# A graph network on one core: SyncE also fetches one tile in 48 of the pair pass, by one-row transfers into four slots of their own

## The reference

```python
h = jnp.maximum(_layernorm(x, axis=-1), 0.0)
hihj = jnp.concatenate([x[src], x[dst]], axis=-1)                       # x is h in here
exp_e = jnp.exp(_silu(_bn(hihj @ Wf + bf, f_gamma, f_beta)))
we = weight[src] * exp_e
a = we / segment_sum(we, dst, num_segments=N)[dst]
z = jnp.einsum('ed,hdk->ehk', hihj, Wg) + bg
z = _silu(_bn(z, g_gamma, g_beta))
h = segment_sum((a[:, :, None] * z).reshape(E, -1), dst, num_segments=N)
out = _bn(h, n_gamma, n_beta) + x
```

## Time and profile before

| | |
|---|---|
| median of 3 runs | 11156.53 us (11154.51 to 11157.13) |
| the profiled execution | 11159.11 us |
| its span, first to last instruction | 11157.3 us |
| GpSimd busy over the span | 8098.3 us, 73% |
| PE, PEld, VectorE, ScalarE busy | 4270.1, 2948.2, 3430.3, 3212.6 us |
| mean granted TensorE clock | 0.596 |
| the gathers of the three passes in parts | 4596, busy 4348.0 us |
| of the pass with weights | 1532, busy 1454.6 us |
| of the pair pass | 1563, busy 1496.6 us |

### The profile page before, as it was taken

One profiled execution on the slowest core, in us unless ns is written; L12 is line 12 of the kernel. 1 busy time (PEld: TensorE's weight loads), 2 busy tenths in 40 slices (PEclk: granted clock), 3 DMA queues, 4 the chain that ended last, 5 costly groups with the idle time before them and its releaser, 6 DMA issues. The chain is left out here.

```text
span 11157.3 us, 112702 instructions
## 1 busy us (share of the span) xinstructions
PE 4270.1 (38%) x19462; PEld 2948.2 (26%) x19462; DVE 3430.3 (31%) x7386; ACT 3212.6 (29%) x7261; POOL 8098.3 (73%) x8241
## 2 busy tenths in 40 slices
PE   1222222342222233333333433343464333443687
PEld 0111111121111112111111333333353333333576
DVE  4000001110001112000001422222245677777898
ACT  3333333343333334333333300000031111111465
POOL 4777777657777775777777677777766777777676
PEclk5555555665555555555555555556675555555899
DMA  4333333233333333333333222222214555555444
GB/s 105 81 81 81 81 81 81 76 88 81 81 81 81 81 81 102 81 81 81 81 81 81 59 54 54 54 54 54 54 48 148 159 162 163 166 166 170 149 167 134
DMA packets 702798, 1071.72 MB, mean 96 GB/s; under 512 B 164740, under 2 KB 547065, under 8 KB 675209
## 3 DMA queue, kind: packets, MB, share of 16 engines
q0 software_dynamic: 323616, 664.87, 23.0%
q10 hardware_dynamic: 247712, 225.10, 6.1%
q1 hardware_dynamic: 130793, 174.77, 4.9%
HBM read 904.67 MB, written 161.05 MB: 96 GB/s over the span
## 5 line engine op out<-in xcount | busy, mean ns | idle before, releaser
L460 POOL DMA_INDIRECT big<-table_parts,tile_cols x4596 | 4348.0, 946 | 1563.2 <-issue 1400.2
L641 PE MATMUL psum<-big 128*128 x4992 | 1722.0, 505 | 3998.4 <-SPq L472 3044.2
L641 PEld LDWEIGHTS psum<-big 128*128 128x128 bf16 x4992 | 670.0, 141 | 4980.6 <-issue 2814.6
L460 POOL DMA_INDIRECT big<-ptable,tile_cols x1563 | 1496.6, 957 | 498.4 <-issue 476.0
L460 POOL DMA_INDIRECT big<-table,tile_cols x1532 | 1454.6, 949 | 469.5 <-issue 467.0
L596 ACT ACTIVATE big<-big,ones 128x2048 bf16<-128x2048 bf16 x312 | 624.4, 2001 | 3573.5 <-PE psum L641 2381.1
L589 ACT ACTIVATE big<-iota_col,dl_tab 128x128 bf16<-128x128 f32 x4992 | 1490.7, 387 | 32.9 <-PEq L765 12.5
L1656 PE MATMUL psum<-acc,big 128*128 x3328 | 785.0, 419 | 1205.5 <-DVE big L1632 1193.4
L618 DVE TENSOR_REDUCE acc<-psum 128x128 f32<-128x384 f32 (+1 forms) x196 | 109.7, 560 | 3558.1 <-PE psum L644 1783.4
L713 PE MATMUL psum<-big 128*128 x3328 | 754.6, 419 | 1158.3 <-SPq L472 619.7
L1656 PEld LDWEIGHTS psum<-acc,big 128*128 128x128 f32 x3328 | 701.8, 315 | 1288.5 <-issue 1288.2
(11 more groups left out here) (301 smaller groups left out, 4278.8 us busy)
## 6 DMA issues: line engine op xcount, KB each, us to landing
big<-table_parts SPq DMA_DIRECT2D x11904, 0.8 KB
big<-dl_rows ACTq DMA_DIRECT2D x104, 1024.0 KB
zrows<-big ACTq DMA_DIRECT2D x104, 1024.0 KB, 5.5
big<-zrows SPq DMA_DIRECT2D x104, 1024.0 KB, 4.9
big<-table_parts,tile_cols POOLq DMA_INDIRECT x4596
big<-table SPq DMA_DIRECT2D x3968, 0.5 KB
table_parts<-big SPq DMA_DIRECT2D x42, 672.0 KB, 3.5
big<-ptable,tile_cols POOLq DMA_INDIRECT x1563
```

The lines of the kernel that those rows point to most:

```text
L460: pool.indirect_dma_start(out=slots[:, t % (groups * GT), 0:width], out_offset=None, in_=tab, in_offset=bass.IndirectOffsetOnAxis(ap=idx_t ...
L641: last = nc.tensor.matmul(held, m, rows_t, start=False, stop=False, skip_group_check=True)
```

## The change

The pair pass, too, gives the last tile of every sixth group to SyncE. Its list, `Z_SIDE`, has 32 groups (8 to 194), one more than `SIDE`, since the ring is shorter. The row numbers are copied a third time into `side_tab` and multiplied by 520, the bytes of a row of `ptable`. A fetched tile does not go into the ring but into one of four slots of its own, `z_side`, which lie behind the work buffer in `big`, at `Z_SIDE_AT`. So the table of slots needs other entries for the items of these tiles: nine further small operations of VectorE in setup find whether a tile is a fetched one (a division by 48 by a multiplication and a shift), which of the four slots it has, and add the difference to `slot_at`. VectorE then addresses all of `big` with the table. The relaying, the ring and the passes 0 to 3 stay.

```diff
+    Z_SIDE = list(range(SIDE_FIRST, TGROUPS - Z_RGROUPS + Z_LEAD + 1, SIDE_EVERY))
+    Z_SIDE_SLOTS, SIDE_TILES = 4, SIDE_EVERY * GT
+    SIDE_SHIFT, SIDE_FACTOR, SIDE_FROM = 16, -(-(1 << 16) // SIDE_TILES), 2
+    SIDE_OFFSET = SIDE_FROM * SIDE_TILES - SIDE_FIRST * GT - GT + 1
...
+        Z_SIDE_AT = RB + OB + WB
+        z_side = big[:, Z_SIDE_AT:Z_SIDE_AT + Z_SIDE_SLOTS * ACW].rearrange("p (u f) -> p u f", f=ACW)
...
-        side_tab = sb("side_numbers", [64 + len(SIDE), P], i32)
-        side_of = [side_tab[64 * k:64 * k + len(SIDE), :] for k in range(2)]
+        side_tab = sb("side_numbers", [64 + len(Z_SIDE), P], i32)
+        side_of = [side_tab[32 * k:32 * k + len(Z_SIDE), :] for k in range(3)]
...
-            return no < PASSES - 1 and g in SIDE
+            return g in (SIDE if no < PASSES - 1 else Z_SIDE)
...
-                if k >= len(SIDE):
+                if k >= len(SIDE if no < PASSES - 1 else Z_SIDE):
                     return
-                t = SIDE[k] * GT + GT - 1
+                t = Z_SIDE[k] * GT + GT - 1
+                slot = t % RSLOTS if no < PASSES - 1 else (k + SIDE_FROM) % Z_SIDE_SLOTS
...
-                    sp.dma_start(slots[e:e + 1, t % RSLOTS, 0:width], flat[:, bass.ds(at, width)]).then_inc(s_side, 16)
+                    sp.dma_start(slots[e:e + 1, slot, 0:width], flat[:, bass.ds(at, width)]).then_inc(s_side, 16)
...
-                dve.wait_ge(s_last, 64)
+                dve.wait_ge(s_last, 16 * (2 + len(side_of)))
                 nc.vector.tensor_scalar(side_of[0], side_of[0], 2 * NPARTS * F, None, ALU.mult)
+                nc.vector.tensor_scalar(side_of[2], side_of[2], 4 * ACW, None, ALU.mult)
...
+                nc.vector.tensor_scalar(side_n, tile_f, float(SIDE_OFFSET), float(SIDE_FACTOR), ALU.add, ALU.mult)
...
+                nc.vector.tensor_scalar(side_q, side_n, SIDE_SHIFT, None, ALU.arith_shift_right)
...
+                nc.vector.scalar_tensor_tensor(side_is, side_q, -float(SIDE_TILES), tile_f, ALU.mult, ALU.add)
+                nc.vector.tensor_scalar(side_n, side_q, Z_SIDE_SLOTS - 1, None, ALU.bitwise_and)
...
+                nc.vector.tensor_scalar(side_is, side_is, -float(SIDE_OFFSET), None, ALU.is_equal)
+                nc.vector.scalar_tensor_tensor(side_step, side_n, float(ACW), slot_at, ALU.mult, ALU.subtract)
...
+                nc.vector.scalar_tensor_tensor(side_is, side_q, float(SIDE_FROM), side_is, ALU.is_ge, ALU.mult)
...
+                nc.vector.scalar_tensor_tensor(side_step, side_step, float(Z_SIDE_AT), side_is, ALU.add, ALU.mult)
...
+                nc.vector.tensor_tensor(slot_at, slot_at, side_step, ALU.add)
...
-                relay_rows(sp, no, Z_RGROUPS, Z_LEAD, s_added, PSLOTS)
+                relay_rows(sp, no, Z_RGROUPS, Z_LEAD, s_added, PSLOTS, side_rows(no, ptable, z_side, ACW, 2, 4 * ACW))
...
-                    slots = pair_values(dve, SLOT, q, (SLOTS - 1) * ACW)
+                    slots = pair_values(dve, SLOT, q, Z_SIDE_AT + (Z_SIDE_SLOTS - 1) * ACW)
...
-                        last = nc.vector.scalar_tensor_tensor(zbuf[:, h, u, 0:ACW], dyn(ring_flat, slots[u], ACW), in_win[:, h, u:u + 1],
+                        last = nc.vector.scalar_tensor_tensor(zbuf[:, h, u, 0:ACW], dyn(big[:, :], slots[u], ACW), in_win[:, h, u:u + 1],
```

More of the change, by code:

```diff
@@ L81, in gnn_kernel @@
     SIDE_SPAN = SIDE_EVERY * GT * P
+    Z_SIDE = list(range(SIDE_FIRST, TGROUPS - Z_RGROUPS + Z_LEAD + 1, SIDE_EVERY))
+    Z_SIDE_SLOTS, SIDE_TILES = 4, SIDE_EVERY * GT
+    SIDE_SHIFT, SIDE_FACTOR, SIDE_FROM = 16, -(-(1 << 16) // SIDE_TILES), 2
+    SIDE_OFFSET = SIDE_FROM * SIDE_TILES - SIDE_FIRST * GT - GT + 1
+    assert all((t + SIDE_OFFSET) * SIDE_FACTOR >> SIDE_SHIFT == (t + SIDE_OFFSET) // SIDE_TILES for t in range(NI))
+    assert (NI + SIDE_OFFSET) * SIDE_FACTOR < 1 << 24 and Z_LEAD == LEAD
     SIDE_BASE = (SIDE_FIRST + 1) * GT * P - SIDE_SPAN
-    assert SIDE_FIRST == RGROUPS and RGROUPS - SIDE_EVERY == LEAD and SIDE_BASE + len(SIDE) * SIDE_SPAN <= E
+    assert SIDE_FIRST == RGROUPS and RGROUPS - SIDE_EVERY == LEAD and SIDE_BASE + len(Z_SIDE) * SIDE_SPAN <= E
+    assert len(SIDE) <= len(Z_SIDE) <= 32 and max(Z_SIDE) * GT + GT < NT
     CHUNKS = NW // CW
@@ L161, in gnn_kernel @@
         SMALL_AT = RB + OB + WB + 224
+        Z_SIDE_AT = RB + OB + WB
+        z_side = big[:, Z_SIDE_AT:Z_SIDE_AT + Z_SIDE_SLOTS * ACW].rearrange("p (u f) -> p u f", f=ACW)
+        assert Z_SIDE_SLOTS * ACW <= 224 + 11 * (NW + 1)
         assert ONE_AT + BODY * P <= SMALL_AT and STAT_AT + NPARTS * NI // 2 <= SMALL_AT + 11 * (NW + 1)
@@ L325, in gnn_kernel @@
         ring_field_at = small[:, 7, 2 * CW + 2 * IG:2 * CW + 3 * IG]
+        side_q, side_n = (small[:, 7, 2 * CW + k * IG:2 * CW + (k + 1) * IG].bitcast(i32) for k in (3, 4))
+        side_is, side_step = small[:, 7, 2 * CW + 5 * IG:2 * CW + 6 * IG], small[:, 9, RG + 6 * IG:RG + 7 * IG]
+        assert 2 * CW + 6 * IG <= NW + 1 and RG + 7 * IG <= NW + 1
         plan_t = onehot_flat[0:IG, 4 * P:4 * P + P // HALF * PLAN_WORDS].bitcast(i32).rearrange("g (a k) -> g a k", k=PLAN_WORDS)
@@ L832, in _ @@
                     sp.sem_inc(s_last, 16)
-                side_src = src[SIDE_BASE:SIDE_BASE + len(SIDE) * SIDE_SPAN].rearrange("(k s) -> k s", s=SIDE_SPAN)[:, SIDE_SPAN - P:]
+                side_src = src[SIDE_BASE:SIDE_BASE + len(Z_SIDE) * SIDE_SPAN].rearrange("(k s) -> k s", s=SIDE_SPAN)[:, SIDE_SPAN - P:]
                 for to in side_of:
```

## The result

The changed kernel takes 11254.53 us (median of 4 runs, 11246.11 to 11263.56) against 11155.52 us: a ratio of 1.0089, 95% interval 1.0076 to 1.0102. It is 99 us slower, where 36 us faster was forecast, and 4.5 us above the range.

What follows compares the result with a forecast made beforehand. GpSimd's gather issue rate was taken to bound the pair pass: -40.4 (gathers) + 3 (dearer gathers) + 1 (setup) = -36.4 us from 11159.1, so 11122.7, or 11120 as median of the runs; range 11110 to 11250.

Steps and rivals of the forecast that it cites:

- The bound before, and the 40.4 us of the gathers: Pair pass: GpSimd's issue rate, 1.262 us a tile, sets it; 32 gathers fewer take 40.4 us off.
- Side rows making gathers dearer, taken at 3 us: Pair pass: SyncE's row transfers could make each remaining gather dearer; bounded at 8 us, taken as 3.
- Slots, VectorE: Pair pass: reading rows from the new slots costs nothing; VectorE as next bound stays hidden, giving 7.4 of 31.0 us waits.
- Setup, taken at 1 us: Setup: ten more small VectorE operations and one more load of 32 rows cost 1 to 2 us, taken as 1.
- SyncE keeps about 220 us free: SyncE in the pair pass: 1607 us for 32 tiles, 1712 with old work, of the new 1932 us.
- I take the setup's row: SyncE's rows beside 1 MB stores: 0.27 instead of 0.225 us an issue, as in setup; 42 us lost.
- my upper bound: SyncE beside ScalarE's 104 stores: no transfer issued during 520 us, losing 400 us, with the loads 493.
- The last row "I take nothing": SyncE's wait for a fetched tile's last row, 1.2 us in the pass with weights: taken as no cost.
- My bound of 1 us a tile: SyncE's wait for a tile's last row: upper bound of its cost, 32 us in all.
- The ring is too short: Rival, 4-group ring: late releases make GpSimd wait; no change, 11150 to 11157; chance 0.09 together with VectorE.
- SyncE as the bound: Rival, pair pass: rows held fourfold in stores make SyncE the bound; slower, about 11290 or 11390; chance 0.20.
- The Trainium skill: DMA queues: engines take turns by packet, so stores would cost rows nothing; same sum, SyncE some 40 us more free.

Runs made afterwards that it cites:

- e9: Changed kernel with only two of ScalarE's 104 stores of pair values, the message pass rereading those two: 11115.29 us, ratio 0.9967 to the kernel before.
- e1: Changed kernel with SyncE fetching one tile in 56 (27 tiles, every seventh group) in the pair pass: 11129.01 us, ratio 0.9971 to the kernel before.
- e2: Changed kernel with SyncE fetching one tile in 96 (16 tiles) in the pair pass: 11143.4 us, ratio 0.9984 to the kernel before.
- e12: Changed kernel's setup and patched slot table, but GpSimd gathers all 1563 tiles and SyncE fetches none in the pair pass: 11156.61 us, ratio 1.0002.
- e11: Changed kernel waiting for last rows an iteration later, with two alternating semaphores and 31 tiles from groups 9, 15, ...: 11169.03 us, ratio 1.0014.
- e4: Changed kernel with GpSimd also gathering SyncE's 32 tiles, so SyncE's rows are extra: 11249.1 us, ratio 1.0078 to the kernel before.
- e3: Changed kernel with ScalarE's 1 MB stores in 8 KB pieces from another tile, pair values not stored: 11191.35 us, ratio 1.0027.
- e5: Changed kernel with only the first two of 104 stores, on the slow chip: 14277.93 us, ratio 0.9948 to the kernel before there.
- e6: Kernel before the change with only the first two stores, on the slow chip: 14360.79 us, ratio 0.9991 to the kernel before there.
- e8: Changed kernel with last-row waits an iteration later (31 tiles, two semaphores), on the slow chip: 14297.79 us, ratio 0.9957 to the kernel before there.
- e10: Kernel before the change with only two stores, rerun as the control: 11151.29 us, ratio 0.9997 to the kernel before.

## Why the prediction was wrong

- *The bound before, and the 40.4 us of the gathers*: right. e9 against its control gives 36, e1 31 of 34, e2 17 of 20.
- *Side rows making gathers dearer, taken at 3 us*: nothing; 957 ns before and after. *Slots, VectorE*: right (e12). *Setup, taken at 1 us*: not contradicted; the first gather of all starts at 267.5 us instead of 267.0.
- *"SyncE keeps about 220 us free"* is the step that failed, with the losses that were set against it. First, waits were counted as free time, the 38.3 us for last rows in the pass with weights among them. A wait for a row just issued is not free time, since nothing else on that queue can run in it. In the pair pass it is 84.7 us, 2.65 a tile and not the 1.2 that I read, and the landings of the first groups take 34.5 us that are not free either. Second, the work without stores measured 1735 us, not 1712. So 1932 - 1735 - 85 - 35 = 77 us were free, not 220.
- *"I take the setup's row"*: mis-sized, and the largest error. I took 42 us for the row transfers and 60 for the loads beside the stores, about 100. Against e9 the row transfers cost 167 us and the loads 39, together 206. The setup's transfer was issued beside a queue that was stuck, not beside a store out of SBUF, and it was the wrong neighbour. The nearer row was the load of the earlier trace rows, 3550 ns for 856, a factor of 4; the issues went from 225 to 1006 ns, a factor of 4.5. A load and an issue by the same queue in the same stretch suffered alike. But the slow issues are few, some four a store, so that a store costs 2.0 us and not the 5 us of my upper bound.
- A loss of 206 us by the durations against 77 us free leaves 129 us by which the pass should be longer than 1932; it is 2057 - 1932 = 125. (With the 203 us of the difference of work it would be 126, but that figure is taken from the length of the pass itself and proves nothing.)
- *The last row "I take nothing"*: wrong. The waits are 84.7 us in all, and nearly all of it is length of the pass: 2.4 of 2.65 us a tile come back in e11. My bound of 1 us a tile was passed too. I asked only whether GpSimd's release came in time, for which the slack was enough, and not what the wait takes from a queue with hardly any time to spare.
- *The ring is too short*: refuted by e1 and e4. In e1, e2 and e9, with the same ring of 4 and the same fetches between releases, GpSimd does not wait for a release once; here the short ring costs something only when SyncE is behind on average.
- *The rival that came true* was mine, SyncE as the bound, at 0.20 and with 11290 for a threefold-and-more slowdown of issues over all of the 520 us. Its sign and mechanism were right, and the forecast itself had the sign wrong; 11254 comes from a smaller slowdown (206 us and not 393) plus the waits that it lacked. That its 11290 is only 35 us off is these two errors against each other, and so luck.
- The Trainium skill, "DMA: Bandwidth & Descriptors", section "Queues, rings and completion order", lets each DMA engine take turns between queues. The trace does not bear this out between SyncE's queue and ScalarE's either: of the 1621 packets from 9191 to 9194 ScalarE's queue has 1617 and SyncE's 3, while four of SyncE's issues stand in that window; the software queue, on which GpSimd issues three gathers there, has none. So landing suffers as well as issue: the waits for last rows are 84.7 us with the stores and 64.0 without them, the longest 4.2 us in both. The larger loss is in the time that an issue takes on SyncE, about which that rule says nothing.

Open: what in a store makes an issue of another queue slow. It is not mainly the number of pieces (e3). The gathers are not the cause: the pass with weights has them and no issue over 338 ns. The 1 MB loads of `dl_rows` do it a little (e9), the stores do it most. The slow issues fall into the microseconds in which SyncE's queue gets next to no packets, but that the one causes the other was not tried, nor whether it is the reading of SBUF or the writing to HBM.

The best version is e1, under both kernels: seven groups a tile instead of six give SyncE 10 us more for the same 128 rows, 11129 us, 0.3% under the kernel before.

## What to carry to other kernels

An engine that gives work to a neighbour can move the bound there. Add up the neighbour's whole cycle, its own waits for what it has just issued included, and compare it with the cycle of the engine that you relieve; here it came to 63.4 us against 59.3. Issue costs are to be taken from a stretch with the same traffic, and if the queue's other instructions (here the small loads) slow down beside it, expect the same of the issues.

To find out whether the relieved engine is still the bound, give it its old work back (e4): if the time does not move, it is not.

## What the runs showed of the hardware that was not expected

A one-row transfer issued by SyncE takes 225 ns in the median and up to 1006 (1057 over the pass) behind a 1 MB store from SBUF to HBM that ScalarE has issued; of 203 issues over 600 ns 190 start 1 to 4 us behind such a store; a load of 32 numbers into registers takes 5003 ns at most where 2.1 us is its median. For 3 us of a store 1617 of 1621 packets are ScalarE's, 3 SyncE's and none of the software queue.

One chip ran the kernel before 29% slower, and e5, e6 and e8 28 to 29% slower than e9, e10 and e11, the same kernels elsewhere. The kernel of e6 in its pair pass there: the gathers, TensorE's idle time, and GpSimd's waits, then the same idle time of TensorE in e10:

```profile
L460 POOL DMA_INDIRECT big<-ptable,tile_cols x1563: 941/947/1269, 10959.8 to 13572.9; - x196
...
PEld psum L1656 <- issue: 1833.0, 295, 22.8
...
POOL big L460 <- SPq L483: 639.4, 65, 18.7
POOL big L460 <- issue: 477.5, 1497, 2.7
...
PEld psum L1656 <- issue: 1263.6, 309, 10.4
```

A gather still takes 941 to 1269 ns. TensorE's idle time before weight loads, with nothing that the profile shows, is 1833 us there and 1264 in e10, up to 22.8 and 10.4 us at a time, and GpSimd waits 639.4 us for releases where in e10 it never does. A register move of SyncE takes up to 1409 ns in e5, against 37 in e9. On that chip both kernels with fetches, e5 and e8, were faster than before by 0.4 to 0.5%, while the kernel of e8 was 0.14% slower than before on the other chip (e11). The cause was not looked for.
